# A three-layer perceiver kernel: output stored tile by tile, the output projection's bias added once, four idle products fewer

## The chip, the cores and the metric

One core of a Trainium2 chip. The metric is device time in microseconds of one execution. TensorE (PE) multiplies, VectorE (DVE), ScalarE (ACT) and GpSimd (POOL) do the elementwise work, SyncE (SP) issues nearly all transfers.

## The reference, cut to what matters

```python
# x: (8, 64, 256), ctx: (8, 1601, 256); 16 heads of 16
def xattn(q, ctx):                      # cross attention
    s = einsum('bhqd,bhkd->bhqk', (q @ Wq.T + bq), (ctx @ Wk.T + bk)) / 4
    o = softmax(s) @ (ctx @ Wv.T + bv)
    return o @ Wo.T + bo                # bo: the output projection's bias
x = x + xattn(layernorm(x), ctx)
x = x + causal_attention(layernorm(x), keys and values from the same rows)
n = layernorm(x)
p = softmax(n @ Wg + bg); top 2 of 8 experts
x = x + sum_k p_k * (gelu(n @ W1[e_k] + b1[e_k]) @ W2[e_k] + b2[e_k])
```

## The kernel before, in words

The 512 rows are four tiles of 128 (two batches each), x_all of 128 x 4 x 256. f32 matrices that need precision are split into a high and a low part of type fp32r, and a product is three products (split_product, L1148). The stages are:

- **Prologue** (FIRST_ORDER): x tile 0 is normalized and transposed; context chunks, key weights and value weights are split; keys (units "K"), values ("V") and the score maxima ("M") of batch 0 are made. PE has nothing to do at first and runs idle products (warm_up, L1372 to L1383): WARM_UP[0] of them before the transposes of x, WARM_UP[1] after them, ahead of the first key product, which waits for the split key weights (wk_lo, L987).
- **Four tile stages** (tile 0 is FIRST, then two MIDDLE, then LAST), each of 26 steps, 13 key tiles for each of two batches. In a step PE opens the scores with the shift (L1331), adds the score products (L1345), and weighs the values with the probabilities of the step before (L1163); ACT takes the exponential (L719); POOL adds the probabilities up (L481), DVE in the very last batch. Between them go "units": products that each fill one bank of a ring of five and are read by ACT or DVE. They make the next batch's keys and values and, for the tile before, the rest of the layers (a chain of units: y1, xt1, qk, ..., y2, ..., router, gt, b2). Tile 0 has no tile before it; its chain makes the queries of the other tiles (p1, r1, ..., r3). Which unit stands in which step is written in tables (REST_CHAIN, CHAIN_AT, CHAIN_AT_LAST, CHAIN_ALONE), and every engine walks its own queue in that order. Step 13 is the first of the second batch.
- **The unit y1** is the cross attention's output projection: two f32 products and, as a third, a product of a row of ones with the bias row (L1232, L1233). The bias row bo_all is bo + bv @ Wo.T, made at the end of the prologue. DVE adds x (L882), takes statistics, and the chain goes on.
- **Last rows and experts**: the last tile's chain (TAIL) runs beside expert 0 on the three finished tiles; then the experts one after another, each in 8 chunks of 128 hidden units: hidden (fills h), gelu on ACT, split on DVE, output (adds into two banks of 2 x 256 columns, one for each pair of tiles). y_chunk counts the chunks; once an expert's last chunk is done, gated_sum (L1074) adds gate times output to x_all for the four tiles. The last expert's is alone at the end (L1142, L1143), followed by one store of x_all on SP (L531 to L533).

Of the kernel before, what the change touches and what calls it, by code (L numbers as in the profile page):

```python
# [9 lines left out]
ALU = mybir.AluOpType  # L10
AX = mybir.AxisListType

P = 128
# [76 lines left out]
FIRST_SPLIT = {1: [(0, 1)], 2: [(0, 2)], 4: [(0, 3)], 9: [(1, 0)]}  # L90
FIRST_V_SPLIT_AT = 2
SPLIT_BY_POOL = [(0, 2), (0, 3)]
WARM_UP = (6, 12)
FIRST_TILE_SPLIT = {0: (1, 1), 1: (1, 2)}

REST_STATS_AT = 0
REST_CHAIN = {3: ["p1"], 5: ["r1"], 6: ["p2"], 8: ["r2"], 9: ["p3"], 11: ["r3"]}
SHIFT_AT = KT - 1
FIND_SHIFT_AT = KT - 3
OWN_V = {0: 11, 1: 12}  # L100
# [174 lines left out]
def perceiver_kernel(nc, x, ctx_t, w_t, wg_t, biases, bo_row, bg_row, w1, b1, w2, b2, eye, masks, causal, out):  # L275
    stack = ExitStack()
    with stack:
# [166 lines left out]
        h_split = sem("h_split")  # L444
        y_chunk = sem("y_chunk")
        y_taken = sem("y_taken")
        stored = sem("stored")

        block = stack.enter_context(nc.Block())
# [36 lines left out]
        @block.sync  # L486
        def _(sp):
            sp.dma_start(x_all[:, 0:1, :], x[:, 0:1, :]).then_inc(x_in, 16)

            def load(b, c):  # L490

                if not (is_first(b) and c < 2):

                    sp.wait_ge(ctx_lo_done, b * NC + c - 1)
                sp.dma_start(ctx_raw[:, c % 2, :, 0:EDGE[c + 1] - EDGE[c]],
                             ctx_t[b, :, :, EDGE[c]:EDGE[c + 1]]).then_inc(ctx_in[c % 2], 16)

            def load_expert(e, i):
                sp.dma_start(raw_sb[i][:, 0], w1[e]).then_inc(w_in[i], 16)
                sp.dma_start(raw_sb[i][:, 1], w2[e]).then_inc(w_in[i], 16)  # L500

            sp.dma_start(ident[:, :], eye).then_inc(consts_in, 16)
            sp.dma_start(bias_sb[:, :, :], biases).then_inc(consts_in, 16)
            load(0, 0)
            sp.dma_start(w_raw[:, 0], w_t[:, 6]).then_inc(k_weights_in, 16)
            sp.dma_start(w_sb[:, 0], w_t[:, 0]).then_inc(weights_in, 16)
            load(0, 1)
            sp.dma_start(w_raw[:, 1], w_t[:, 7]).then_inc(v_weights_in, 16)
            for dst, src in ((bo_sb[:, :], bo_row), (bg_sb[:, :], bg_row), (wg_sb[:, :, :], wg_t),
                             (b1_sb[:, :, :], b1), (b2_sb[:, :], b2), (causal_sb[:, :], causal)):  # L510
                sp.dma_start(dst, src).then_inc(late_in, 16)
            load(0, 2)
            sp.dma_start(x_all[:, 1:TT, :], x[:, 1:TT, :]).then_inc(rest_in, 16)
            load(0, 3)
            sp.dma_start(w_sb[:, 1:6], w_t[:, 1:6]).then_inc(late_in, 16)
            for c in range(NC):
                load(1, c)
            with sp.Fori(1, TT) as t:
                for bi in range(2):
                    for c in range(NC):  # L520
                        load(2 * t + bi, c)

            sp.wait_ge(scores_done, (B - 1) * KT + LAST_V_AT + 2)
            load_expert(0, 0)
            load_expert(1, 1)
            with sp.Fori(1, E // 2) as p:
                for i in range(2):

                    sp.wait_ge(w_split, (2 * p + i - 1) * 2 * PIECES)
                    load_expert(2 * p + i, i)  # L530
            sp.wait_ge(y_taken, E)  # L531
            sp.dma_start(out, x_all[:, :, :]).then_inc(stored, 16)
            sp.wait_ge(stored, 16)  # L533


        @block.gpsimd
# [51 lines left out]
        def _(act):  # L588
# [14 lines left out]
            def unit(units, n, kind, u, t, b, parity):  # L603
                if kind[0] == "r" and kind != "router":
                    units.wait_filled(act, filled, n)
                    queries_hi(bank[:, units.bank_of(n), :], int(kind[1]))
                    return
                if kind == "M" or kind in ("y1", "s0", "s1", "o0", "o1", "y2", "b2"):
                    return
                src = bank[:, units.bank_of(n), :]  # L610
                units.wait_filled(act, filled, n)
# [175 lines left out]
        def _(dve):  # L787
# [53 lines left out]
            def queries_lo(src, t, done):  # L841

                dve.wait_ge(q_hi_done, G * t + G)
                for g in range(G):
# [2 lines left out]
                        scalar=bias_sb[:, 0, g:g + 1], in1=q_hi[:, 2 * t:2 * t + 2, g, :].bitcast(F32), op0=ALU.add,  # L847
                        op1=ALU.subtract).then_inc(q_split if g < G - 1 else done, 1)

            def unit(units, n, kind, u, t, b, parity):  # L850
                src = bank[:, units.bank_of(n), :]
                if kind[0] == "r" and kind != "router":
# [22 lines left out]
                if kind == "M":  # L875
                    c, g, j, width = unit_of_max(u)
                    nc.vector.tensor_reduce(maxes[:, g * PAIRS + j, c:c + 1], src[:, 0:width], AX.X,  # L877
                                            ALU.max).then_inc(read_dve, 1)
                elif kind in ("y1", "y2"):

                    x_tile = x_all[:, bass.ds(t, 1), :].rearrange("p a n -> p (a n)")
                    nc.vector.tensor_tensor(x1[:, :], src[:, 0:D], x_tile if kind == "y1" else x1[:, :],  # L882
                                            ALU.add).then_inc(read_dve, 1)
# [255 lines left out]
                experts(p, True)  # L1139
            links[:] = [start + (E // 2 - 2) * per, 0]  # L1140
            experts(E // 2 - 1, False)
            dve.wait_ge(y_chunk, chunk_of_all(E, 0))  # L1142
            gated_sum(E - 1, 0, TT, 6)  # L1143


        @block.tensor
        def _(pe):
# [41 lines left out]
            def unit(units, n, kind, u, t, b, parity):  # L1189
# [38 lines left out]
                elif kind == "y1":  # L1228

                    pe.wait_ge(o_ready, 2 * t + 2)  # L1230
                    for g in range(G):
                        nc.tensor.matmul(dst[:, 0:D], o_t[:, g, :], w_sb[:, 1, g, :], start=(g == 0), stop=False)  # L1232
                    ins = nc.tensor.matmul(dst[:, 0:D], ones_f[0:1, :], bo_all[:, :], start=False, stop=True)  # L1233
                elif kind[0] == "p":
                    pe.wait_ge(xn_ready, int(kind[1]) + 1)
                    ins = transposes(dst)
# [198 lines left out]
                              [((w[0][:, d, cols], w[1][:, d, cols]), (xn2_hi[:, d, toks], xn2_lo[:, d, toks]))  # L1435
                               for d in range(DC)]).then_inc(h_psum, 1)

            def output(i, c, n, at, first, last):


                pe.wait_ge(h_split, n + 1)
# [1 line left out]
                for t in range(first, last):  # L1443
# [2 lines left out]
                                        [((h_hi[:, c % 4, toks], h_lo[:, c % 4, toks]),  # L1446
                                          (w_hi[i][:, 1, cols], w_lo[i][:, 1, cols]))],
                                        start=(c == 0 and (t % 2 == 0 or t == first)), stop=(c == HC - 1), skip_group_check=True)
                ins.then_inc(y_chunk, 1)

            def alone(s):
                for n, kind, u in TAIL.at[s]:
# [61 lines left out]
            with pe.Fori(1, E // 2) as p:  # L1514
                experts(p)
            for c in (HC - 2, HC - 1):
                output(1, c, chunk_of_all(E - 1, c), 6, 0, TT)


# [41 lines left out]
```

## Time and profile before

| | us |
|---|---|
| median of 3 runs (lowest, highest) | 676.38 (676.06, 677.6) |
| the profiled execution | 677.73 |
| its span, first to last instruction | 675.9 |
| PE busy | 648.0 |
| DVE / ACT / POOL busy | 472.3 / 326.6 / 298.5 |
| mean granted clock of TensorE | 0.992 |

Busy times are those of one execution; a matmul's busy time overlaps that of its neighbours, so the spacing of their starts tells their rate.

### The profile page before, as it was taken

Reading aid. Unit: us, or ns where it says so; the run is one execution under the profiler, and the core shown is the slowest. Engines: PE = TensorE matmul, PEld = TensorE weight load, DVE = VectorE, ACT = ScalarE, POOL = GpSimd, SP = SyncE. Lnnn points to the kernel's source line nnn. Section 1 sums busy time; section 2 is a strip of 40 time slices with the busy share of each in tenths; the row PEclk is TensorE's granted clock in tenths of the full one; section 3 lists DMA queues with packets and bytes.
Section 4 is the critical chain, followed back from the end, with each engine's and each line's share of the span. In section 5 each row is a group of like instructions: output and inputs, shape, how many; then the busy total and the mean of one; then the engine's idle time right before and its main releaser. Section 6 shows DMA issues by size and latency. Waiting matters only on the chain.

```text
span 675.9 us, 15772 instructions
## 1 busy us (share of the span) xinstructions
PE 648.0 (96%) x6410; PEld 532.6 (79%) x6418; DVE 472.3 (70%) x870; ACT 326.6 (48%) x533; POOL 298.5 (44%) x386
## 2 busy tenths in 40 slices
PE   7989999999999989999998999888999999999996
PEld 4778878778868867877886886656789999999996
DVE  4887757676759787585877865668777567667653
ACT  4355655654554554554455544355544444444421
POOL 1137797996766788596668758200000000000000
PEclk9999999999999999999999999989999999999999
DMA  5411110100010010010000000053003302330000
GB/s 164 147 47 53 31 46 26 50 26 25 27 50 2 26 50 25 27 50 26 27 25 26 1 2 1 22 230 126 1 1 126 124 10 118 124 124 0 0 0 32
DMA packets 12852, 34.11 MB, mean 50 GB/s; under 512 B 1515, under 2 KB 9972, under 8 KB 10612
## 3 DMA queue, kind: packets, MB, share of 16 engines
q1 hardware_dynamic: 12756, 33.19, 14.8%
q8 instruction: 47, 0.77, 0.5%
q14 instruction: 17, 0.14, 0.1%
q0 software_dynamic: 32, 0.01, 0.0%
HBM read 32.67 MB, written 0.52 MB: 49 GB/s over the span
## 4 chain that ended last, share of the span: by engine, by line
PE 78%; DVE 9%; issue 5%; POOL 5%; ACT 2%; DMA 0%; POOLq 0%; DVEq 0%; ACTq 0%
PE bank L1154 44%; PE bank L1163 9%; PE bank L1345 9%; POOL prob_sum L481 5%; PE bank L1331 4%; PE bank L1224 3%; PE bank L1264 2%; PE bank L1273 2%; DVE prob_sum L481 1%; DVE maxes L877 1%; DVE ctx_lo L465 1%; ACT k_hi L615 1%; PE bank L1248 1%; DVE k_lo L858 1%; PE bank L1375 1%
## 5 line engine op out<-in xcount | busy, mean ns | idle before, releaser
L481 POOL TENSOR_TENSOR prob_sum<-probs,prob_sum 128x256 f32<-128x256 f32 x336 | 268.5, 830 | 73.6 <-ACT probs L719 68.2
L719 ACT ACTIVATE probs<-bank 128x1024 f32<-128x1024 f32 (+1 forms) x104 | 106.7, 1026 | 115.3 <-PE bank L1345 102.2
L877 DVE TENSOR_REDUCE maxes<-bank 128x1 f32<-128x400 f32 (+1 forms) x256 | 129.4, 564 | 22.7 <-PE bank L1224 22.3
L701 ACT ACTIVATE h_raw<-bank,b_sb 128x512 f32<-128x512 f32 (+2 forms) x72 | 46.2, 642 | 106.7 <-PE bank L1154 106.6
L1154 PE MATMUL bank<-w_hi,h_hi 128*128 128x256 f32 x256 | 72.6, 284 | 0.0
L1154 PE MATMUL bank<-w_hi,h_lo 128*128 128x256 f32 x256 | 72.1, 282 | 0.0
L1154 PE MATMUL bank<-w_lo,h_hi 128*128 128x256 f32 x256 | 72.0, 281 | 0.0
L858 DVE SCALAR_TENSOR_TENSOR k_lo<-bank,bias_sb,k_hi 128x400 fp32r<-128x400 f32 (+2 forms) x64 | 40.4, 631 | 44.6 <-ACT k_hi L615 44.6
L1163 PE MATMUL bank<-probs,v_sb 128*32 128x128 f32 (+1 forms) x1664 | 68.3, 283 | 2.5 <-DVE masked L812 2.0
L1345 PE MATMUL bank<-qbd_hi,k_hi 64*128 64x256 f32 (+1 forms) x416 | 67.8, 321 | 0.0
L1154 PE MATMUL bank<-wv_hi,ctx_hi 128*128 128x256 f32 (+1 forms) x208 | 65.1, 313 | 2.7 <-DVE maxes L877 2.4
L1088 DVE CAST h_hi<-h_raw 128x512 fp32r<-128x512 f32 (+2 forms) x72 | 28.4, 395 | 52.8 <-ACT h_raw L701 51.7
L1345 PE MATMUL bank<-qbd_lo,k_hi 64*128 64x256 f32 (+1 forms) x416 | 59.6, 281 | 0.0
L1345 PE MATMUL bank<-qbd_hi,k_lo 64*128 64x256 f32 (+1 forms) x416 | 59.5, 281 | 0.0
L1224 PE MATMUL bank<-k_hi,qbd_hi 64*128 64x400 f32 (+1 forms) x256 | 58.4, 443 | 1.0 <-DVE qbd_hi L838 0.4
L618 ACT ACTIVATE v_sb<-bank 128x256 f32<-128x256 f32 (+1 forms) x104 | 39.7, 382 | 40.2 <-PE bank L1154 36.8
L1154 PE MATMUL bank<-wv_lo,ctx_hi 128*128 128x256 f32 (+1 forms) x208 | 58.4, 281 | 0.0
L1154 PE MATMUL bank<-wv_hi,ctx_lo 128*128 128x256 f32 (+1 forms) x208 | 58.1, 280 | 0.0
L615 ACT ACTIVATE k_hi<-bank,bias_sb 128x400 fp32r<-128x400 f32 (+2 forms) x64 | 38.1, 596 | 40.2 <-PE bank L1154 40.2
L1163 PEld LDWEIGHTS bank<-probs,v_sb 128*32 128x32 f32 (+1 forms) x1664 | 39.8, 110 | 18.8 <-issue 6.2
L1154 PE MATMUL bank<-xn_hi,w_lo 128*128 128x512 f32 (+2 forms) x144 | 54.4, 378 | 0.0
L1154 PE MATMUL bank<-xn_hi,w_hi 128*128 128x512 f32 (+2 forms) x144 | 54.3, 377 | 0.0
(157 smaller groups left out, 1420.9 us busy)
## 6 DMA issues: line engine op xcount, KB each, us to landing
raw<-in_w SPq DMA_DIRECT2D x16, 1024.0 KB, 6.8
ctx_raw<-in_ctx_t SPq DMA_DIRECT2D x16, 400.0 KB, 3.6
ctx_raw<-in_ctx_t SPq DMA_DIRECT2D x8, 402.0 KB, 3.8
ctx_raw<-in_ctx_t SPq DMA_DIRECT2D x8, 399.0 KB, 3.5
w_sb<-in_w_t SPq DMA_DIRECT2D x1, 1280.0 KB
w_raw<-in_w_t SPq DMA_DIRECT2D x2, 256.0 KB, 4.8
result<-x_all SPq DMA_DIRECT2D x1, 512.0 KB, 3.0
x_all<-in_x SPq DMA_DIRECT2D x1, 384.0 KB, 4.4
```

What stands on the lines that cost most here:

```text
L481: ins = engine.tensor_tensor(prob_sum[0:ROWS[k], cols], probs[0:ROWS[k], s % 2, cols], acc[0:ROWS[k]], ALU.add)
L615: nc.scalar.activation(k_hi[parity][:, g, EDGE[c]:EDGE[c + 1]], src[:, EDGE[c] - CH[c]:CW], ACT.Identity, bias=bias_sb[:, 1, g:g + 1]).the ...
L618: nc.scalar.activation(v_sb[0:ROWS[u], u * D:u * D + D], src[0:ROWS[u], 0:D], ACT.Copy).then_inc(read_act, 1)
L701: nc.scalar.activation(h_raw[:, c % 2, 0:width], bank[:, at, 0:width], ACT.Gelu, bias=b1_sb[:, bass.ds(e, 1), c:c + 1].rearrange("p a b -> ...
L719: nc.scalar.activation(probs[0:ROWS[k], s % 2, :].rearrange("p (g n) -> p g n", g=G), bank[0:ROWS[k], score_bank(b, k):score_bank(b, k) + ...
L858: nc.vector.scalar_tensor_tensor(out=k_lo[parity][:, g, EDGE[c]:EDGE[c + 1]], in0=src[:, EDGE[c] - CH[c]:CW], scalar=bias_sb[:, 1, g:g + 1 ...
L877: nc.vector.tensor_reduce(maxes[:, g * PAIRS + j, c:c + 1], src[:, 0:width], AX.X, ALU.max).then_inc(read_dve, 1)
L1088: link(nc.vector.tensor_copy(h_hi[:, c % 4, 0:width], h_raw[:, c % 2, 0:width]))
L1154: last = nc.tensor.matmul(dst, lhs, rhs, start=(start and n == 1), stop=(stop and n == 3 * len(pairs)), **more)
L1163: ins = nc.tensor.matmul(dst_bank[32 * j:32 * j + 32, (at + g) * P:(at + g + 1) * P], lhs(g, j), p_rows[:, m * P:(m + 1) * P], start=(star ...
L1224: ins = nc.tensor.matmul(dst[:, 0:width], qbd_hi[rows, parity, g, 2 * i:2 * i + 2, :].rearrange("p s q -> p (s q)"), k_hi[parity][rows, g, ...
L1345: ins = nc.tensor.matmul(bank[0:rows, score_bank(b, k) + r, g * RH * Q:(g + 1) * RH * Q], stays, moves, start=False, stop=(part == 2), ski ...
```

## The change

Three things. WARM_UP[1] falls from 12 to 8. The bias product leaves y1; instead a unit "bias" in step 13 of tile 0's stage multiplies ones by bo_all once, and DVE adds the bank to all four tiles of x_all; y1 on DVE waits until that has happened. The last output chunk of the last expert signals bank by bank (y_bank), DVE sums tile by tile, and SP stores each tile when it is summed. The scores still open with the shift, as before.

```diff
-WARM_UP = (6, 12)
+WARM_UP = (6, 8)
-REST_CHAIN = {3: ["p1"], 5: ["r1"], 6: ["p2"], 8: ["r2"], 9: ["p3"], 11: ["r3"]}
+REST_CHAIN = {3: ["p1"], 5: ["r1"], 6: ["p2"], 8: ["r2"], 9: ["p3"], 11: ["r3"], 13: ["bias"]}
...
-            sp.wait_ge(y_taken, E)
-            sp.dma_start(out, x_all[:, :, :]).then_inc(stored, 16)
-            sp.wait_ge(stored, 16)
+            for t in range(TT):
+                sp.wait_ge(y_taken, E + t)
+                sp.dma_start(out[:, t:t + 1, :], x_all[:, t:t + 1, :]).then_inc(stored, 16)
+            sp.wait_ge(stored, 16 * TT)
...
+            bias_added = FIRST.before[2] + FIRST.counts(1 + next(n for s in range(STEPS) for n, kind, _ in FIRST.at[s]
+                                                                 if kind == "bias"))[2]
...
+                elif kind == "bias":
+                    dve.wait_ge(xn_ready, TT)
+                    nc.vector.tensor_tensor(x_all[:, :, :], x_all[:, :, :],
+                                            src[:, 0:D].unsqueeze(1).broadcast_to([P, TT, D]), ALU.add)\
+                        .then_inc(read_dve, 1)
                 elif kind in ("y1", "y2"):
+                    if kind == "y1":
+                        dve.wait_ge(read_dve, bias_added)
...
-            dve.wait_ge(y_chunk, chunk_of_all(E, 0))
-            gated_sum(E - 1, 0, TT, 6)
+            for t in range(TT):
+                dve.wait_ge(y_bank, t // 2 + 1)
+                gated_sum(E - 1, t, t + 1, 6)
...
-                        nc.tensor.matmul(dst[:, 0:D], o_t[:, g, :], w_sb[:, 1, g, :], start=(g == 0), stop=False)
-                    ins = nc.tensor.matmul(dst[:, 0:D], ones_f[0:1, :], bo_all[:, :], start=False, stop=True)
+                        ins = nc.tensor.matmul(dst[:, 0:D], o_t[:, g, :], w_sb[:, 1, g, :], start=(g == 0),
+                                               stop=(g == G - 1))
+                elif kind == "bias":
+                    ins = nc.tensor.matmul(dst[:, 0:D], ones_f[0:1, :], bo_all[:, :], start=True, stop=True)
...
+                    if by_bank and t % 2:
+                        ins.then_inc(y_bank, 1)
+                if not by_bank:
+                    ins.then_inc(y_chunk, 1)
...
-                output(1, c, chunk_of_all(E - 1, c), 6, 0, TT)
+                output(1, c, chunk_of_all(E - 1, c), 6, 0, TT, c == HC - 1)
```

## Rows read from the trace of the kernel before

**Rows 1.** The page: the chain that ended last, by engine, by line.
```profile
PE 78%; DVE 9%; issue 5%; POOL 5%; ACT 2%; DMA 0%; POOLq 0%; DVEq 0%; ACTq 0%
```

**Rows 2.** Busy time by stretch: stretch, length, engines, clock, DMA share, GB/s.
```profile
10.30:38.00 27.70, 25.56 (x145) 19.67 (x144) 22.22 (x43) 11.59 (x23) 4.43 (x3) 1.00 0.34 118
...
124.00:238.00 114.00, 111.98 (x1312) 89.30 (x1316) 81.90 (x138) 58.77 (x91) 86.02 (x111) 1.00 0.11 31
...
465.00:515.00 50.00, 48.34 (x374) 40.64 (x375) 36.59 (x89) 23.97 (x48) 1.10 (x2) 1.00 0.21 75
```

**Rows 3.** The start in order of time: start, length, engine, line, operation.
```profile
5.62 4.93 PE L1375 MATMUL bank<-ones_bf 128*128 128x512 bf16 x12
...
8.09 0.69 DVE L987 TENSOR_TENSOR wk_lo<-w_raw,wk_hi 128x512 fp32r<-128x512 f32 x1
...
9.46 0.15 PEld L1375 LDWEIGHTS bank<-ones_bf 128*128 128x128 bf16 x1 [0.28 <-issue]
...
9.88 0.15 PEld L1375 LDWEIGHTS bank<-ones_bf 128*128 128x128 bf16 x1 [0.28 <-issue]
...
10.19 0.53 PE L1154 MATMUL bank<-ctx_hi,wk_hi 128*128 128x402 f32 x1
...
10.56 0.34 PE L1154 MATMUL bank<-ctx_lo,wk_hi 128*128 128x402 f32 x1
...
11.29 0.35 PE L1154 MATMUL bank<-ctx_hi,wk_lo 128*128 128x402 f32 x1
```

**Rows 4.** Chain (start, length, what), then DVE's timeline, about step 13.
```profile
88.56 4.29 POOL prob_sum L481 x4
...
92.97 2.81 POOL prob_sum L481 x4
...
95.83 0.69 PE bank L1163 x16
...
94.49 0.64 DVE L858 SCALAR_TENSOR_TENSOR k_lo<-bank,bias_sb,k_hi 128x402 fp32r<-128x402 f32 x1 [2.94 <-ACT k_hi L615]
...
96.55 0.48 DVE L811 TENSOR_SCALAR masked<-bank,mask_sb 128x256 f32<-128x256 f32 x1 [1.42 <-PE bank L1163]
```

**Rows 5.** The end in order of time, and two transfers: KB, us to landing.
```profile
669.72 0.28 PE L1154 MATMUL bank<-w_hi,h_lo 128*128 128x256 f32 x1
...
670.44 0.28 PE L1154 MATMUL bank<-w_hi,h_lo 128*128 128x256 f32 x1
670.76 1.66 DVE L1077 SCALAR_TENSOR_TENSOR x_all<-bank,gates,x_all 128x256 f32<-128x256 f32 x4 [2.42 <-PE bank L1154]
672.44 0.36 SPq L532 DMA_DIRECT2D result<-x_all  x1
...
result<-x_all SPq DMA_DIRECT2D x1, 512.0 KB, 3.0
...
x_all<-in_x SPq DMA_DIRECT2D x1, 128.0 KB, 2.2
```

**Rows 6.** Timeline, then busy time by stretch (columns of rows 2), last batch.
```profile
448.90 0.27 PE L1306 MATMUL bank<-ident,gate_tile 128*8 128x128 f32 x1 [2.94 <-DVE gate_tile L930]
...
463.92 1.22 DVE L481 TENSOR_TENSOR prob_sum<-probs,prob_sum 65x1024 f32<-65x1024 f32 x1
...
450.30:457.10 6.80, 6.80 (x68) 4.69 (x66) 4.14 (x7) 3.09 (x4) 0.00 (x0) 0.50 0.00 0
```

**Rows 7.** PE in order of time around a y2 (L1294) and a y1 (L1232).
```profile
223.78 1.03 PE L1294 MATMUL bank<-w_sb,o_t 128*128 128x256 f32 x4
...
224.76 0.28 PE L1154 MATMUL bank<-wv_lo,ctx_hi 128*128 128x256 f32 x1
...
266.16 1.02 PE L1232 MATMUL bank<-w_sb,o_t 128*128 128x256 f32 x4
...
267.96 0.28 PE L1154 MATMUL bank<-wv_lo,ctx_hi 128*128 128x256 f32 x1
```

**Rows 8.** DVE in order of time: a probability sum of 1024 columns, last batch.
```profile
449.47 1.22 DVE L481 TENSOR_TENSOR prob_sum<-probs,prob_sum 128x1024 f32<-128x1024 f32 x1
```

More of the change, by code:

```diff
@@ L446, in perceiver_kernel @@
         y_taken = sem("y_taken")
+        y_bank = sem("y_bank")
         stored = sem("stored")
@@ L607, in unit @@
                     return
-                if kind == "M" or kind in ("y1", "s0", "s1", "o0", "o1", "y2", "b2"):
+                if kind in ("M", "bias", "y1", "s0", "s1", "o0", "o1", "y2", "b2"):
                     return
@@ L1436, in hidden, with output @@
                                for d in range(DC)]).then_inc(h_psum, 1)
-            def output(i, c, n, at, first, last):
+            def output(i, c, n, at, first, last, by_bank=False):
                 pe.wait_ge(h_split, n + 1)
@@ L1448, in output @@
                                         start=(c == 0 and (t % 2 == 0 or t == first)), stop=(c == HC - 1), skip_group_check=True)
-                ins.then_inc(y_chunk, 1)
+                    if by_bank and t % 2:
+                        ins.then_inc(y_bank, 1)
+                if not by_bank:
+                    ins.then_inc(y_chunk, 1)
             def alone(s):
```

## The prediction

> **What bounds the kernel now.** I read the page first: TensorE (PE) carries 78% of the chain of waits, DVE 9%, POOL 5% [rows 1]. The busy time by stretch says the same: in a tile stage PE stands idle for 2.0 of 114 us, and beside expert 0 for 1.7 of 50 [rows 2]. So an instruction taken off PE in those stages should shorten the span, unless GpSimd (POOL), which adds up the probabilities and is busy 86.0 of those 114 us, is late next. Three places are not simply PE-bound: the start, where PE runs idle products until the first weights are split [rows 3]; one stretch of the first tile, where POOL's sums are the chain [rows 4]; and the end, where the last sums and one store follow the last product [rows 5]. The clock comes last: a stretch from 450.3 to 457.1 us was granted half of it [rows 6].
>
> **Part 1, idle products at the start, 12 to 8.** The twelve take 4.93 us from 5.62 on, and their weight loads are 0.42 to 0.43 us apart, which for 512 columns is the 1.2 GHz level. The page's clock line stands at its highest digit there, so the level is read from the spacing. The first key product K0 is therefore begun at 10.19, although its last input, wk_lo, is done at 8.09 + 0.69 = 8.78 [rows 3]. With eight, the idle products end at 5.62 + 8 x 0.427 = 9.04, still behind 8.78, so the removed time is not taken by a wait. Four products are 1.71 us. But K0 now starts at the low level: 402 columns at 1.2 GHz are 0.335 us, where the rows show 0.18 to 0.19 between products from 10.56 on. If the clock rises at the same moment, shortly before 10.3, three or four products run slow: 9.04 + 3 x 0.335 + 3 x 0.185 = 10.60, against 11.29 + 0.18 = 11.47 before. That is 0.87; I take **0.85**. After it PE and DVE are busy 25.6 and 22.2 of 27.7 us, each fed by the other's results on K0 and what follows it [rows 2], so the stretch should move as a whole. Ends: 0 (an input is late after all) and 1.7 (the clock is high at once).
>
> **Part 2, the bias.** Each of the four y1 units ends in a one-row f32 product, two passes. How much PE time is that? The unit y2 is the same product without it. From the first pass of y1 to the second product of the V unit behind it pass 267.96 - 266.16 = 1.80 us; for y2 it is 224.76 - 223.78 = 0.98 [rows 7]. So the bias costs 0.82 us a unit, more than two of the four passes that take 1.02 together, probably since the array drains on both sides. Four units: 3.28. Of these, three lie in the tile stages, where the chain goes through y1 and the V product behind it, and the fourth lies in the last stretch beside expert 0, where PE is idle 1.7 of 50 us [rows 2]. Here it also shortens the wait of VectorE (DVE) for y1, which then feeds statistics, normalize and transposes; the next late thing there is PE's own queue.
>
> Added is one such product in step 13 of tile 0 (0.82), and on DVE one add of 128x1024 from PSUM. A DVE add of 1024 columns takes 1.22 us [rows 8]. Where do they fall? DVE's k_lo of that step ends at 94.49 + 0.64 = 95.13 and DVE then waits until 96.55: 1.42 us in which the 1.22 fit [rows 4]. If that cover is gone, it costs up to 1.2. PE's 0.82 fall between K0 and the value product, 92.8 us. POOL is the chain from 88.56 to 92.97 + 2.81 = 95.78, but PE reaches the denominators at 95.83 after barely any wait [rows 4], so almost all of the 0.82 comes out behind POOL's end. I charge it in full; the ends are 0 and 0.82 + 1.2 = 2.0. The wait added before y1 is for an add that ran 50 us earlier and holds up nothing. The ring of banks turns by one unit: a unit still reuses the bank of the fifth before it, so only five units see another neighbour. Net: 3.28 - 0.82 = **2.46**. Ends: 4 x 0.51 (the passes alone) - 2.0 = 0, and 3.3.
>
> POOL's four pieces take 4.29 us in one step and 2.81 in the next [rows 4]. The slow ones lie beside DVE operations with both inputs in SBUF (ctx_lo, spreading the queries). If the bias add does the same to POOL, it adds up to 4.29 - 2.81 = 1.5 us to a chain that runs beside PE. The Trainium skill ("GPSIMD Engine Reference", Key points) says that GpSimd contends with DVE instructions that have two SBUF inputs or a 2-port mode. The bias add has one of its inputs in PSUM, so by that rule the extra is nothing and the sum stands; without the rule it would be up to 1.5 us later. No row of before shows this very operation.
>
> **Part 3, the end.** The last chunk issues twelve products 0.12 us apart; the sixth starts at 669.72, the twelfth at 670.44, and DVE starts 0.32 us after the latter, at 670.76. Its four sums end at 672.42 and SyncE (SP) issues at 672.44 [rows 5]. With a signal for each bank DVE can start at 669.72 + 0.32 = 670.04; four sums of (672.42 - 670.76) / 4 = 0.415 end at 671.70, and the bank of the last two is full at 670.76, before DVE comes to it at 670.87. The last issue is 0.72 us earlier. SP issues four stores at the pace of the sums; one issue took 0.36, so the last finds SP free. Landing: 3.0 us for the 512 KB store, 2.2 us for the 128 KB load of x [rows 5]; a load stands in for a store that the trace doesn't show at this size. I take 0.73 of the 0.8. Together **1.45**. Ends: 0.3 (landing as before, with 0.4 lost to SP's queue) and 1.6.
>
> **Sum.** 0.85 + 2.46 + 1.45 = 4.76 us. The profiled execution took 677.73 (span 675.9 and 1.83 around it), so it would come to 672.97. The median of the three runs is 676.38, 1.35 below the profiled one; from it the forecast is **671.6**. The scores that open with the shift are untouched: 0.
>
> **Rivals.**
> *Absorbed:* the y1 savings in the three tile stages don't come through, since POOL's sums or a DVE link is late next. For it: POOL's chain in [rows 4] and its busy share. Against: the chain passes over PE at each y1, and POOL waits for ACT's exponentials, which wait for PE. Then only the last y1 counts: 0.85 + 0.82 - 0.82 + 1.45 = 2.3, 674.1 us.
>
> *A low-clock stretch goes:* from 450.3 to 457.1 the granted clock was 0.50, after PE had stood idle 2.94 us for the gates; DVE's sums of this stretch are two rows, in [rows 6, 8]. Six intervals of these sums took 463.92 - 449.47 = 14.45 us. An interval holds a sum of 1.22 and a split of w of about the half of it (1.8 in all), so 6 x 1.8 = 10.8 would do: 3.6 us. Everything there comes 2.5 us earlier now, so the gap may fall differently. For it: three runs and the profile differ by 1.67 us, more than steady work explains. Against: the gap itself stays. 671.6 - 3.6 = 668.0.
>
> *The clock stays low at the start (the other side):* with four fewer idle products the clock doesn't rise at 10.3 but much later. PE is busy 25.56 of 27.7 us after 10.3 [rows 2], so a microsecond at half rate costs 0.46. Slower than before from 4.76 / 0.46 = 10.3 us of extra low clock on, which is until 20.6. If until 24: 671.6 + 13.7 x 0.46 = 677.9. For it: from 450.3 the level stayed low through 6.8 us of unbroken work [rows 6]. Against: K0, the queries and K1 follow the idle products without a gap until 13.6, so PE is no less busy than before, and the 4.93 us of idle products led up to the rise here. The Trainium skill ("TensorE: Matmul & The Clock Gate", Part 1) has the gate follow how busy the engine has recently been, which speaks against it too.
>
> *Nothing much happens:* the start waits for an input, POOL takes the bias, only the earlier issue of the store is left: 676.38 - 0.7 = 675.7.
>
> **How the numbers follow.** Forecast 0.60, absorbed 0.16, low stretch gone 0.12, nothing much 0.08, clock stays low 0.04. Faster by over 0.2% (1.35 us, about what a measurement of this kernel can tell from no change): the first three, 0.88; same 0.08; slower 0.04. The range takes in the absorbed case with half a microsecond (674.6), and below, with the bias and the store at their good ends (0.8 + 0.15) and part of the low stretch, goes to 669.0; it leaves out most of the full 668.0, the unchanged case and the slow one.
>
> **What would show it.** In the profile after: the first L1154 near 9.05 and the first q_hi near 11.7; y1 followed by the V product after about 0.7 us; the denominators of batch 0, near 95, about 0.8 us behind POOL's last piece; the sum of x_all in two pairs, the first beginning before the last product; the last store issued 1 us after the last product and landing in 2.2. Wrong would be: a wait of PE for wk_lo, POOL pieces above 0.75 us beside the new add, a landing of 3 us, a span that does not shrink between 124 and 351 us by 0.8 us a tile, or low-clock stretches in other places.

## The result, and the profile after

The kernel after takes 673.63 us, median of 9 executions (670.73 to 674.97); in the same session the kernel before takes 677.56 (676.06 to 678.66). The ratio is 0.9935, 95% interval 0.9914 to 0.9956, so 3.9 us are gained, where 4.8 were forecast. The time lies in the stated range of 669.0 to 674.6, 2.0 above the 671.6 of the forecast. The profiled execution took 674.92, with a span of 673.1.

The page after, its span, PE's busy time and the chain that ended last, by engine (to be held against [rows 1]):

```profile
span 673.1 us, 15769 instructions
...
PE 647.2 (96%) x6408; PEld 533.3 (79%) x6408; DVE 473.2 (70%) x871; ACT 326.8 (49%) x533; POOL 298.4 (44%) x386
...
PE 79%; DVE 10%; issue 5%; POOL 3%; ACT 2%; DMA 0%; POOLq 0%; DVEq 0%; ACTq 0%
```

POOL's share of the chain went from 5% to 3%; otherwise the picture is as before. The start after, in order of time (start, length, engine, line, operation), against [rows 3]:

```profile
5.59 3.62 PE L1393 MATMUL bank<-ones_bf 128*128 128x512 bf16 x8
...
8.27 0.68 DVE L1001 TENSOR_TENSOR wk_lo<-w_raw,wk_hi 128x512 fp32r<-128x512 f32 x1
...
9.01 0.70 PE L1169 MATMUL bank<-ctx_hi,wk_hi 128*128 128x402 f32 x1
9.50 0.50 PE L1169 MATMUL bank<-ctx_lo,wk_hi 128*128 128x402 f32 x1
9.84 0.36 PE L1169 MATMUL bank<-ctx_hi,wk_lo 128*128 128x402 f32 x1
...
10.40 0.35 PE L1169 MATMUL bank<-ctx_hi,wk_lo 128*128 128x402 f32 x1
```

K0 starts at 9.01, runs its first products slow and has its last at 10.40 where it was 11.29: 0.89 us. A y1 with the V products behind it (line L1247 is y1), against [rows 7]:

```profile
152.67 1.02 PE L1247 MATMUL bank<-w_sb,o_t 128*128 128x256 f32 x4
153.34 0.47 PE L1169 MATMUL bank<-wv_hi,ctx_hi 128*128 128x256 f32 x1
153.65 0.28 PE L1169 MATMUL bank<-wv_lo,ctx_hi 128*128 128x256 f32 x1
```

That is 0.98 us from y1's start to the second V product, as y2 had, where y1 took 1.80. Step 13 of the first tile, where the bias now is (L1251 the product, L888 the add, L1178 the denominators), against [rows 4]:

```profile
91.96 0.69 PE L1251 MATMUL bank<-bo_all,ones_f 1*128 1x256 f32 x2
...
94.15 1.21 DVE L888 TENSOR_TENSOR x_all<-x_all,bank 128x1024 f32<-128x1024 f32 x1
95.27 0.65 PE L1178 MATMUL bank<-prob_sum,ones_f 128*32 128x128 f32 x16
...
95.98 0.48 DVE L814 TENSOR_SCALAR masked<-bank,mask_sb 128x256 f32<-128x256 f32 x1 [0.63 <-PE bank L1178]
...
90.06 4.82 POOL L482 TENSOR_TENSOR prob_sum<-probs,prob_sum 128x256 f32<-128x256 f32 x6
96.09 2.33 POOL L482 TENSOR_TENSOR prob_sum<-probs,zero 128x256 f32<-128x256 f32 x4 [1.22 <-PE bank L1178]
```

The add fits in front of the next thing on DVE, which still waits 0.63 us. The denominators start 0.56 us earlier than before (95.83), while K0 had come 0.89 earlier: the added unit costs 0.33. Where the rest of its 0.82 went can be followed on PE: the shift of this step starts 0.09 us earlier than before (94.06 against 94.15), the first product of the score maxima 0.46 (94.10 against 94.56), the last score product 0.35 (95.06 against 95.41) and the denominators 0.56. So two waits of PE, one ahead of the score maxima and one ahead of the denominators, had been there before and were filled. In the trace before the score maxima waited for ACT's k_hi, which came late because ACT's exponential at 92.95 had waited 2.50 us for POOL's sums. The end, against [rows 5], with the stores' size and median landing:

```profile
668.24 0.28 PE L1169 MATMUL bank<-w_hi,h_lo 128*128 128x256 f32 x1
...
668.56 1.66 DVE L1091 SCALAR_TENSOR_TENSOR x_all<-bank,gates,x_all 128x256 f32<-128x256 f32 x4 [1.71 <-PE bank L1169]
...
668.96 0.28 PE L1169 MATMUL bank<-w_hi,h_lo 128*128 128x256 f32 x1
669.08 2.18 SPq L535 DMA_DIRECT2D result<-x_all  x4
...
result<-x_all SPq DMA_DIRECT2D x4, 128.0 KB, 2.0
```

From the last product's start to the end of the span are 673.07 - 668.96 = 4.11 us, before 675.86 - 670.44 = 5.42. The four stores are issued at 669.08, 669.87, 670.27 and 670.74, and the last one is this:

```profile
670.74 0.51 SPq L535 DMA_DIRECT2D result<-x_all  x1
```

DVE's last sum ends at 668.56 + 1.66 = 670.22. So the last store is issued 0.52 us behind its sum, where the single store before was issued 0.02 us behind (672.44 against 672.42): from 669.87 on SP issues without a gap, and the fourth had to wait for those ahead of it.

All this can be added up along one series that both traces have: ACT's 104 exponentials (L719, now L722). The start of each in the trace before less that in the trace after is the lead of the changed kernel at this place:

| place | before | after | lead |
|---|---|---|---|
| first exponential | 42.27 | 41.38 | 0.89 |
| tile 0, step 13 | 92.95 | 92.05 | 0.90 |
| tile 0, step 15 | 100.96 | 100.40 | 0.56 |
| tile 1, step 3 / step 4 (y1 between) | 151.99 / 158.37 | 151.39 / 156.93 | 0.60 / 1.44 |
| tile 2, step 3 / step 4 (y1 between) | 264.88 / 271.25 | 263.48 / 269.01 | 1.40 / 2.24 |
| tile 3, step 2 / step 3 (y1 between) | 374.45 / 379.20 | 372.19 / 376.32 | 2.26 / 2.88 |
| the last | 462.47 | 459.96 | 2.51 |
| last product of the kernel | 670.44 | 668.96 | 1.48 |
| end of the span | 675.86 | 673.07 | 2.79 |

In tile 3 the lead also falls, from 2.90 at step 12 to 2.50 at step 17. Between the last exponential and the last product it should have grown by 0.8, by the fourth y1, and shrank by 1.0. Granted clock by stretch (stretch, length, busy time of each engine, clock, DMA share, GB/s):

```profile
433.20:436.60 3.40, 3.40 (x40) 2.67 (x38) 2.15 (x7) 1.02 (x1) 0.55 (x1) 0.51 0.36 51
446.80:453.70 6.90, 6.90 (x74) 4.81 (x70) 4.17 (x7) 2.49 (x5) 0.00 (x0) 0.51 0.01 4
463.90:467.30 3.40, 3.40 (x13) 3.36 (x12) 2.69 (x6) 0.72 (x2) 0.00 (x0) 0.51 0.78 272
```

The first answers to a stretch that the trace before has from 436.8 to about 440, the second to the row of [rows 6]; the third has no counterpart before. In it the first twelve products of expert 0 run:

```profile
463.77 0.47 PE L1169 MATMUL bank<-xn_hi,w_lo 128*128 128x384 f32 x1
464.04 0.53 PE L1169 MATMUL bank<-xn_hi,w_hi 128*128 128x384 f32 x1
464.36 0.53 PE L1169 MATMUL bank<-xn_lo,w_hi 128*128 128x384 f32 x1
```

They are 0.32 us apart, the 1.2 GHz level for 384 columns. So the profiled execution has one more low-clock stretch than the one it is compared with, and the lead went there. How much of it, and what the fourth y1 gave, is read below from traces without such a stretch.

### The profile page after: what moved, and what is told of

The parts are those of the page before. It is cut to its first block, busy times and chain, and to the rows that moved or that the text cites. A ratio compares the mean times of both kernels' runs of the same rounds, so it can differ in the third digit from the quotient of the medians.

```text
span 673.1 us, 15769 instructions
## 1 busy us (share of the span) xinstructions
PE 647.2 (96%) x6408; PEld 533.3 (79%) x6408; DVE 473.2 (70%) x871; ACT 326.8 (49%) x533; POOL 298.4 (44%) x386
## 4 chain that ended last, share of the span: by engine, by line
PE 79%; DVE 10%; issue 5%; POOL 3%; ACT 2%; DMA 0%; POOLq 0%; DVEq 0%; ACTq 0%
PE bank L1169 45%; PE bank L1363 9%; PE bank L1178 9%; PE bank L1349 4%; PE bank L1239 3%; POOL prob_sum L482 3%; PE bank L1282 2%; PE bank L1291 2%; DVE maxes L883 2%; DVE prob_sum L482 2%; DVE ctx_lo L466 1%; DVE shift L825 1%; ACT k_hi L618 1%; PE bank L1266 1%; DVE k_lo L864 1%
## 5 line engine op out<-in xcount | busy, mean ns | idle before, releaser
L722 ACT ACTIVATE probs<-bank 128x1024 f32<-128x1024 f32 (+1 forms) x104 | 106.7, 1026 | 115.3 <-PE bank L1363 103.2
L1178 PE MATMUL bank<-probs,v_sb 128*32 128x128 f32 (+1 forms) x1664 | 68.3, 283 | 2.5 <-DVE masked L815 2.0
L1178 PEld LDWEIGHTS bank<-probs,v_sb 128*32 128x32 f32 (+1 forms) x1664 | 39.8, 110 | 18.7 <-issue 6.1
```

What stands on the lines that cost most here:

```text
L722: nc.scalar.activation(probs[0:ROWS[k], s % 2, :].rearrange("p (g n) -> p g n", g=G), bank[0:ROWS[k], score_bank(b, k):score_bank(b, k) + ...
L1178: ins = nc.tensor.matmul(dst_bank[32 * j:32 * j + 32, (at + g) * P:(at + g + 1) * P], lhs(g, j), p_rows[:, m * P:(m + 1) * P], start=(star ...
```

## The experiments

### The parts alone

One part of the change at a time, on the kernel before.

```diff
# e1_idle8
-WARM_UP = (6, 12)
+WARM_UP = (6, 8)
```

> Only the first part: the kernel before with 8 idle products in place of 12. Theory (parts add, each at the size that the two traces show): every exponential of the first tile comes 0.9 us earlier than in the trace before and this shift stays the same to the end of tile 3; median 0.9 us lower, so -0.13%, within what separates single runs. Rival (the shift is given back where another engine is late next): 0.9 us at the first exponential, under 0.4 us at the end of the third tile stage. Second rival (the clock rises later with fewer idle products): the first key products stay 0.335 us apart past 10.4 us.

```diff
# e2_bias: the change's bias unit, add and y1; not its WARM_UP, y_bank and four stores
+REST_CHAIN = {..., 13: ["bias"]}
-                    ins = nc.tensor.matmul(dst[:, 0:D], ones_f[0:1, :], bo_all[:, :], start=False, stop=True)
```

> Only the second part: the bias as one product and one add in step 13 of the first tile, y1 without it; 12 idle products and one store as before. Theory: the added unit costs 0.3 us (the exponential of step 14 comes 0.3 us later), because it lies beside the chain of probability sums; each y1 then gives 0.84, 0.84, 0.62 us back; in all 2.0 us by the end of tile 3, and 0.8 us more from the y1 beside expert 0. So -2.8 us, -0.4%. Rival (the sizes of the forecast: the added unit costs 0.82 in full): 0.8 us later at step 14, -2.5 us at the end.

```diff
# e3_store: the change's y_bank and four stores only
+                dve.wait_ge(y_bank, t // 2 + 1)
+                gated_sum(E - 1, t, t + 1, 6)
```

> Only the third part: the last output chunk signals per bank, sums tile by tile, four stores. Theory: from the start of the last product to the end of the span 4.1 us, where the kernel before has 5.5: -1.3 us, the start of the first sum 0.7 us before it was and the rest from a shorter landing. Rival (a store's landing does not depend on its size): 4.8 us, -0.7 us.

| kernel | median us (range) | ratio to before, 95% interval | first exponential | last product to end |
|---|---|---|---|---|
| before, same session | 676.13 (674.63 to 678.40) | | | |
| e1_idle8 | 676.14 (673.13 to 677.66) | 0.9994 (0.9974 to 1.0014) | 41.00 | |
| e2_bias | 674.69 (671.39 to 677.61) | 0.9975 (0.9950 to 0.9999) | 40.59 | 5.41 |
| e3_store | 675.34 (673.20 to 677.05) | 0.9983 (0.9965 to 1.0000) | 42.35 | 4.03 |

The bias part gives 1.4 us by the medians, the store 0.8, the four idle products nothing that the medians show; the intervals of e1 and e3 reach 1 and that of e2 comes to 0.9999, so the medians alone settle little. Executions at a clock of 1.000 show more: before 674.63 to 674.95 (five), e1 673.13 and 673.26, e3 673.20 to 673.59 (three); at 0.992, though, e1 (676.14 to 677.66) lies where before lies. Why so uneven, when the leads inside a trace repeat to 0.05 us? In e2's trace they are 0.40 lost at step 14, then 0.84, 0.83 and 0.62 gained at the three y1, as expected; in e3's the end is 1.39 us shorter, as expected, and its rival (0.7) is refuted. What does not repeat is the clock. Its first rise differs between profiled executions, and with it the start. This is e2, with twelve idle products:

```profile
5.40 2.75 PE L1390 MATMUL bank<-ones_bf 128*128 128x512 bf16 x12
8.60 0.45 PE L1166 MATMUL bank<-ctx_hi,wk_hi 128*128 128x402 f32 x1 [0.44 <-DVE wk_lo L999]
```

The same twelve that took 4.93 us take 2.75, and PE then waits 0.44 us for wk_lo: the clock had risen early, and with that four idle products cost nothing. Over the profiles of this study the first exponential came at 42.27, 40.59 and 42.35 us with twelve idle products, and with eight at 41.38, 41.00, 41.28, 41.01, 40.93, 41.59, 41.68, 41.81, 41.09 and 40.74. The means are 41.74 and 41.25. So the part is worth about 0.5 us on average, which with three profiles against ten that differ by 1 to 1.8 us among themselves is not settled, and 0.9 in a pair like the first. Neither rival of e1 holds: its lead, 1.27 at the first exponential, was 1.36 at the end of the third stage, and its key products were 0.18 to 0.19 us apart from 9.26 us on.

The pair e2 and e3 also shows the fourth y1, since neither trace has a low-clock stretch behind the last exponential, and they differ there by y1 alone. Counted from the last exponential, ACT's third gelu (L701 before) comes at 9.05 us in e3 and at 8.24 in e2: 0.81 less. The fourth comes at 14.62 and 14.34, only 0.28 less, and so do the rest, up to the last (204.14 and 203.85). Between them stand the transposes of the normalized rows, first e3, then e2:

```profile
469.41 0.44 PE L1181 MATMUL bank<-ident,xn 128*128 128x128 f32 x2 [0.16 <-DVE xn L807]
```

```profile
466.83 0.44 PE L1190 MATMUL bank<-ident,xn 128*128 128x128 f32 x2 [0.69 <-DVE xn L806]
```

PE's wait for DVE's normalize grew from 0.16 to 0.69 us: 0.53 of the 0.81 turned into a wait. In the trace after, the last gelu comes 205.02 us behind the last exponential, in e5 (the same kernel, no low stretch there) 203.85. So the third stretch cost it 1.17 us. The 0.8 us that e2's expectation gave the fourth y1 were 0.28.

### Does idle time of PE bring the low clock?

Every execution comes with its mean granted clock. In the first session of experiments the 25 executions of the kernel before were these, by clock:

```
1.000: 674.63 to 674.95 (5)    0.995: 675.26 to 675.96 (5)
0.992: 676.07 to 677.74 (13)   0.988: 678.28, 678.40
```

Four microseconds separate executions of one kernel, as much as the change is worth, and they go with the clock, though not one to one: at 0.992 the times differ by 1.7 us, and the four executions of e2 at 0.990 took 674.75 to 677.61. Where a low stretch falls matters. The traces of e1 and e3, both without one, show what the two stretches of the trace before cost: e3 leads it by 0.07 us in tile 3 at step 12, ahead of both, by 0.28 at step 17, between them, and by 3.29 at the last exponential, behind both; e1 by 1.37, 1.59 and 4.60. The stretch near 437 us cost 0.2 us, the one of 6.8 us 3.0. The first was cheap because the slow products filled time in which PE otherwise waits 1.19 to 1.20 us for DVE's normalize (e1, e3).

Both traces also speak against the obvious cause. This is the wait for the gates and the time behind it in e3 (a product, then the stretch, for PE alone):

```profile
448.62 0.27 PE L1309 MATMUL bank<-ident,gate_tile 128*8 128x128 f32 x1 [2.94 <-DVE gate_tile L932]
...
450.00:457.00 7.00, 7.00 (x126) 1.00 0.01 2
```

The wait is the same 2.94 us as in [rows 6], and the clock stays whole. So the wait alone does not bring the stretch; 17 of the 73 executions of the kernel before in the four sessions of experiments had a mean clock of 1.000, with nothing done about their waits. What the wait can still do is make the stretch more likely, and that is tested next. Here gt and b2 of the last tile stage move two steps back, so that PE has other work while DVE ranks the gates:

```diff
# e4_gates_later (and e11_later), on the changed kernel
-                 11: ["st10", "st11"], 12: ["o0", "o1"], 14: ["y2"], 16: ["xt2"], 17: ["router"], 19: ["gt"],
-                 20: ["b2"]}
+                 11: ["st10", "st11"], 12: ["o0", "o1"], 14: ["y2"], 16: ["xt2"], 17: ["router"], 21: ["gt"],
+                 22: ["b2"]}
```

> The changed kernel with the units gt and b2 of the last tile stage two steps later (21 and 22 in place of 19 and 20), so that TensorE does not stand before the transpose of the gates. Theory (the half-clock stretch of 6.8 us near 450 follows from the 2.9 us for which TensorE stands idle there): the idle time falls under 1.5 us, the half-clock stretch behind it is gone, the time is 2 to 4 us below the changed kernel's, about 670. Rival (half-clock stretches come at random, whatever TensorE does): the stretch stays in some executions and the time stays near 673. Second rival: the idle time only moves to the next wait, for VectorE's probability sums, and stays about 2.9 us long.

670.66 us (669.84 to 670.96), ratio to before 0.9908 (0.9879 to 0.9938). PE by stretch in its trace (stretch, length, busy, clock, DMA share, GB/s):

```profile
440.00:451.00 11.00, 9.86 (x176) 1.00 0.54 226
451.00:460.00 9.00, 6.31 (x124) 1.00 0.00 0
```

No low clock where 6.9 us of it were, and the wait before the gates' product, 2.95 us, is a wait of 1.14 us for gates_t. Two shorter low stretches remain (433 to 436, 460 to 463). The wait for DVE's last sums grew from 1.06 to 1.70 us, so a part of the idle time moved there, as the second rival had it. Part of this gain is the wait itself, so the next experiment moves nothing and only fills the waits, with idle products into the bank that the next unit will take:

```diff
# e6_fill: FILL = (8, 12, 4), on the changed kernel
+            def fill(units, kind, count):
+                n = next(n for s in range(STEPS) for n, other, _ in units.at[s] if other == kind)
+                units.wait_free(pe, read_act, read_dve, n)
+                for _ in range(count):
+                    nc.tensor.matmul(bank[:, units.bank_of(n), :], ones_bf[:, :],
+                                     ones_bf[:, :].unsqueeze(1).broadcast_to([P, 4, P]), start=True, stop=True)
...
+                if b == B - 1 and k == 0:
+                    fill(LAST, "xt2", FILL[0])
...
+                    if units is LAST:
+                        fill(LAST, "gt", FILL[1])
...
+                if b == B - 1:
+                    fill(TAIL, "y1", FILL[2])
```

> The changed kernel once more, beside the others of this call. Theory (the time of an execution is that of its steady work plus what its half-clock stretches cost): executions with a mean granted clock of 0.997 near 671, with 0.992 near 673.7, with 0.989 near 674.7, whatever the median of the day is. Rival (the clock follows the time and not the other way): the same clock with times more than 1.5 us apart.

> The changed kernel with idle products in the three waits of TensorE in the last batch: 8 before it weighs the first values, 12 before the transpose of the gates, 4 before the last denominators; no work is moved. Theory (idle time of TensorE brings the half-clock stretches): no half-clock stretch in the profile, mean clock 0.999 or more in nearly all executions, time 670 to 671, less what the idle products delay (under 0.5 us). Rival (the stretches come from elsewhere): clock 0.989 to 0.997 as before and a time at or above the changed kernel's.

> The changed kernel with gt and b2 two steps later in the last tile stage, and 8 and 4 idle products in the two other waits. Theory: the gains add; no half-clock stretch; about 668.5 us, 2 us under the one with the later gates alone. Rival (the idle time of TensorE near the end of the batch is on VectorE's chain, so that clock there costs nothing): 670.5, as with the later gates alone.

e7 has the later gates and FILL = (8, 0, 4).

| kernel | median us (range) | ratio to before, 95% interval | clock of its executions |
|---|---|---|---|
| before, same session | 676.12 (674.61 to 678.62) | | 0.988 to 1.000 |
| e5, changed kernel again | 671.03 (670.72 to 674.27) | 0.9930 (0.9908 to 0.9952) | 0.989, 0.992 x3, 0.997 x6 |
| e6_fill | 669.45 (669.26 to 674.26) | 0.9890 (0.9851 to 0.9928) | 0.991, 0.999, 1.000 x3 |
| e7_later_fill | 669.28 (668.73 to 670.24) | 0.9888 (0.9848 to 0.9927) | 0.997, 0.999, 1.000 x2 |

Of the changed kernel's 19 executions in two sessions none reached 0.999; with the waits filled four of five did. These four also lie under all ten of e5: adding work that computes nothing made the kernel faster in most executions, though the two intervals overlap. e7's expectation, that the gains of e6 and of the later gates add up to 668.5, missed: its median is only 0.17 us under e6's. e5 also answers the question of the scatter: the clock 0.997 goes with 670.7 to 671.0 us, 0.992 with 673.4 to 673.5, 0.989 with 674.3, as expected to 0.4 us. In these ten the rival's sign, one clock with times more than 1.5 us apart, is absent; it is there in e2 and in the kernel before, as said above. The mean clock orders the executions coarsely.

The one execution of e6 at 0.991 was its profiled one, and it shows where a low stretch can still begin:

```profile
442.18 2.76 PE L1374 MATMUL bank<-ones_bf 128*128 128x512 bf16 x12
445.10 0.27 PE L1327 MATMUL bank<-ident,gate_tile 128*8 128x128 f32 x1 [0.15 <-DVE gate_tile L945]
...
500.00:511.00 11.00, 11.00 (x51) 10.57 (x51) 4.55 (x17) 2.35 (x6) 0.00 (x0) 0.53 0.50 191
```

The wait for the gates is down from 2.95 to 0.15 us, and up to 500 us the clock is whole. Then, at the last tile's chain beside expert 0, it is low for 10 us although PE was busy; its longest wait in the 10 us ahead of it was 0.45 us. From the last exponential to the last gelu e6 takes 208.59 us and e5 203.85, so this stretch cost 4.7 us. A wait of 1 us or more is therefore neither needed for a low stretch nor enough for one (e3). What the runs show is a matter of frequency: with the waits filled (e6, e7, e12) 11 of 15 executions had a clock of 0.999 or more, without filling or later gates (the changed kernel, e5, e9, e10) 2 of 38, with the later gates alone (e4, e11) none of 10. But the kernel before had such a clock in 17 of 73. What decides in a single execution stays open.

### Twelve, eight, none

```diff
# e8_idle0, on the changed kernel
-WARM_UP = (6, 8)
+WARM_UP = (6, 0)
```

> The changed kernel with no idle products between the transposes of x and the first key product (6 and 0). Theory (idle products are only cover for a wait that ends with wk_lo near 8.9 us, and keep the clock): TensorE idles from 5.8 to 8.9, the key products start near 8.9 at the low level and stay there past 11 us; the first exponential comes 0.5 to 2 us later than with 8. Rival (the idle products are of no use): the first exponential comes at the same time or earlier.

673.54 us (672.73 to 676.33), ratio to before 0.9963 (0.9942 to 0.9983). PE waits 3.09 us for wk_lo, and still works at the low level from 11.0 to 14.5 us (a product, then the stretch):

```profile
8.65 0.70 PE L1169 MATMUL bank<-ctx_hi,wk_hi 128*128 128x402 f32 x1 [3.09 <-DVE wk_lo L1001]
...
11.00:14.50 3.50, 3.50 (x15) 3.20 (x13) 1.63 (x3) 1.98 (x4) 0.00 (x0) 0.50 0.29 115
```

The first exponential is at 42.80, 1.4 us behind the changed kernel's, within the expected 0.5 to 2. So idle products are worth their place, and this is what the forecast's rival of a late clock would look like: it cost 1.4 to 2.5 us, not the 4.8 that would have made the change a loss.

### Where the bias unit stands, and one store

```diff
# e9_bias_step19, on the changed kernel
-REST_CHAIN = {..., 13: ["bias"]}
+REST_CHAIN = {..., 19: ["bias"]}
```

> The changed kernel with the bias unit in step 19 of the first tile in place of step 13. Theory (in step 13 most of its 0.82 us lies beside POOL's chain of sums, which sets the pace there; in step 19 TensorE sets it): the shift of the exponentials against the kernel before keeps its value over step 14 and falls by 0.7 to 0.85 us behind step 19, so 0.4 us more than in step 13. Rival (the added unit costs 0.4 us wherever it stands): it falls by 0.3 to 0.45 us.

ACT's exponentials of steps 19 and 20 of the first tile in e9's trace:

```profile
116.18 1.03 ACT L722 ACTIVATE probs<-bank 128x1024 f32<-128x1024 f32 x1 [1.41 <-PE bank L1363]
120.96 1.03 ACT L722 ACTIVATE probs<-bank 128x1024 f32<-128x1024 f32 x1 [0.66 <-PE bank L1363]
```

The trace before has them at 116.78 and 120.75: a lead of 0.60 became -0.21, so the unit costs 0.81 us here. In step 13 it cost 0.33 to 0.36, read from step 16 on (0.90 to 0.57 in the changed kernel, 0.45 to 0.09 in e10). The median, 672.93 us with ratio 0.9935 (0.9915 to 0.9955), cannot tell 0.4 us. Two of e9's nine executions had a clock of 1.000, which none of the changed kernel's had, and took 669.99 and 670.27; the kernel before took 674.69 to 674.87 at that clock in the same session. With no low stretch on either side the change is thus worth 4.4 to 4.9 us, even with the unit in its dearer place. That is more than the parts measured in the traces add up to, and why is open.

```diff
# e10_one_store, on the changed kernel
-                sp.wait_ge(y_taken, E + t)
-                sp.dma_start(out[:, t:t + 1, :], x_all[:, t:t + 1, :]).then_inc(stored, 16)
+            sp.wait_ge(y_taken, E + TT - 1)
+            sp.dma_start(out, x_all[:, :, :]).then_inc(stored, 16)
```

> The changed kernel with its sums per bank, but one store of all four tiles at the end. Theory (sums 0.7 us earlier, and a 512 KB store lands later than a 128 KB one by 0.8 to 1.0): from the start of the last product to the end of the span 4.8 us, where the changed kernel has 4.1 and the kernel before 5.5. Rival (the store's size does not matter, all of the gain is the earlier sums): 4.1 to 4.3 us.

```profile
667.97 0.28 PE L1167 MATMUL bank<-w_hi,h_lo 128*128 128x256 f32 x1
...
669.26 0.36 SPq L533 DMA_DIRECT2D result<-x_all  x1
...
result<-x_all SPq DMA_DIRECT2D x1, 512.0 KB, 3.0
```

The span is 672.70, so last product to end takes 4.73 us. Of the 1.31 us gained at the end, 5.42 - 4.73 = 0.69 are the earlier sums and 4.73 - 4.11 = 0.62 the small stores. These land in 1.7 to 2.1 us where 512 KB take 3.0, so they would give about 1; the rest is lost because the last of them is issued 0.52 us behind its sum and not 0.02. The median is 672.91, ratio 0.9957 (0.9934 to 0.9980).

### A version that beats both

Later gates with and without idle products in the two other waits.

> The changed kernel with the later gates once more, beside the one with idle products added. Theory (idle time brings the stretches, and two waits are left without cover): clock between 0.992 and 0.998, 670.6. Rival (the two waits do no harm): the same time as with the idle products, within 0.5 us.

> The same with 8 and 4 idle products in the two waits. Theory: clock 0.999 or more in most executions, 669.0 to 669.5, 1.2 us under the one without them. Rival: within 0.5 us of it.

| kernel | median us (range) | ratio to before, 95% interval | clock |
|---|---|---|---|
| e11_later | 670.04 (669.60 to 671.02) | 0.9906 (0.9887 to 0.9925) | 0.994 to 0.997 |
| e12_later_fill | 669.20 (668.53 to 670.08) | 0.9896 (0.9877 to 0.9916) | 0.997 x2, 1.000 x4 |

Both beat the kernel before by 7 to 8 us in their session (677.35). The second is 0.84 us lower by the medians, less than the 1.2 expected, and the two intervals overlap, so that the idle products add something to the later gates is likely and not settled; four of its six executions kept a clock of 1.000, none of the other did. Against the changed kernel, 671.0 and 673.6 us in its two sessions, the comparison runs over the kernel before, and there too the intervals touch; but all six executions of e12 (up to 670.08) lie under all nineteen of the changed kernel (from 670.72).

## Why the prediction was right, point by point

- **Idle products, 0.85.** Right for the pair of traces, 0.89, with K0 started at 9.01 (9.04 forecast) and its first products slow. As a step for the time of a typical execution it was too large: it took the clock's rise in one trace, shortly before 10.3 us, as fixed. Over the profiles it is 0.5 (three against ten of them, so a rough figure), and e1's medians show nothing.
- **y1 without the bias, 4 x 0.82.** Measured 0.84, 0.84 and 0.62 (e2: 0.84, 0.83, 0.62). The third was mis-sized: in the last tile stage y1 is followed by the value weighing, not by a V product, and I had priced all four with the V product behind. The fourth gave 0.28. That the one-row product costs more than its two passes because the array drains on both sides was a guess that no run tests. For the fourth the failed step is "the next late thing there is PE's own queue": next late is DVE's normalize, 0.53 us of new wait.
- **The added unit, 0.82 in full.** Measured 0.33. The step that failed is that PE's 0.82 would come out almost whole behind POOL's end. PE reached the denominators 0.05 us behind POOL's last sum because it had itself been waiting: 0.26 us up to the last score product and 0.21 ahead of the denominators (0.35 less 0.09, and 0.56 less 0.35, in the comparison of step 13). The denominators now start 95.27 - 94.88 = 0.39 us behind POOL's last piece, where 0.8 were forecast. e9 shows that the full price, 0.81, is paid where POOL is not the chain.
- **POOL beside the add.** It was not slowed: six pieces took 4.82 us across the step, the last ending at 94.88, exactly 0.90 us before its counterpart (95.78), which is the lead of that place. Only the last piece ran beside the add; it took 0.74 us, and single pieces at 62.59 and 125.63 us of the trace before took 0.73. The Trainium skill ("GPSIMD Engine Reference", Key points) names contention with DVE instructions that have two SBUF inputs or a 2-port mode. That this add, with one input in PSUM, is outside the rule was the prediction's reading, and the one piece agrees with it.
- **The end, 1.45.** Measured 1.31: 0.69 for the sums (0.72 forecast) and 0.62 for the four stores (0.73). The second hides two errors that nearly cancel. The landing got shorter by about 1.0 us (1.7 to 2.1 against 3.0), more than the forecast 0.73; the load of x, 2.2, was a fair stand-in. And "the last finds SP free" failed: one issue took 0.36 us alone but the later ones 0.35 to 0.51, and the last store left 0.50 us later behind its sum than before. The last store was issued 1.78 us after the last product's start, not 1.
- **The sum, 4.76, and the rivals.** The terms as measured are 0.5 (0.89 in the pair), then 0.84 + 0.84 + 0.62 + 0.28, less 0.33, and 1.31: 4.1 (4.5). That the y1 gains were forecast 0.7 too large and the added unit's cost 0.5 too large nearly cancels, and that is luck. The time is 2.0 us above the forecast, 1.2 of it because the kernel before took 677.56 beside it and not 676.38, and 0.8 because less was gained. In the pair of traces 2.79 us were gained and not 4.5: low-clock stretches took back 0.39 in tile 3 and 1.17 behind it, and 0.15 more is unexplained. Executions at equal clock agree: in e5's session 677.4 to 677.8 before against 673.4 to 673.5 after, both at 0.992, 4.2 apart. The absorbed rival is refuted for the three tile stages: each lead gained at a y1 was still there at the next one. It holds for the fourth, where it was not looked for. The rival of the low-clock stretch priced it at 3.6 us; e1 and e3 show 3.0. It tied the stretch to PE's wait of 2.94 us for the gates, and those two traces have the wait without the stretch. In the trace after it did not go, and one came in addition (463.9 to 467.3), which the prediction had named as a sign of being wrong, and took 1.17 us. The rival of a clock that stays low did not come: the key products ran at the full rate from 9.84 us on. Medians of 3.9 and 5.1 us gain in two sessions lie on both sides of the forecast, since the share of executions at each clock differs.

## What to carry to other kernels

Read the scatter of a kernel's executions together with their mean granted clock before pricing a change of half a percent: here the clock moved single executions by 4 us, and moving or filling TensorE's waits of 1 to 3 us was worth 1.6 to 1.8 us by the medians of one session. Look also for traces that have the suspected cause without the effect: two single-part experiments had the same wait and no low clock. Price an instruction by the distance between its neighbours in two otherwise equal places, and look which neighbour stands behind each copy. An instruction that has to be added belongs where another engine sets the pace: the same unit cost 0.33 us there and 0.81 elsewhere. An instruction that starts right behind another engine's result may have been waiting for it: its start does not show how much slack its own engine has.

## What the runs showed of the hardware that I had not expected

- Idle products in TensorE's waits raised the mean granted clock of most executions from 0.989 to 0.997 up to 0.999 or 1.000 and took 1.6 us off the median in the same session (671.03 to 669.45).
- The moment at which the clock first rises differs between executions of one program: twelve idle products took 4.93 us in one and 2.75 us in another.
- With no idle products ahead, TensorE's key products ran at half clock until past 14.5 us, after it had idled 3.09 us ahead of them.
- A low-clock stretch of 10 us began at 500.4 us in e6 while TensorE was busy, and cost 4.7 us. A stretch of about 3.4 us cost only 0.2 where TensorE would otherwise have waited 1.2 us for VectorE (the first of the trace before, against e1 and e3).
- A wait of TensorE of 2.94 us was followed, 1.4 us later, by 6.8 us at half clock in one execution (the trace before), and by none in two others (e1, e3).
- A 512 KB store took 3.0 us to land from 128 partitions of 4 KB; four of 128 KB, issued 0.4 to 0.8 us apart, took 1.7 to 2.1 us each. Issued back to back, one occupied SyncE for 0.35 to 0.51 us.
